# A decoder layer on one core: one more key-half add on VectorE, feed-forward tiles over the score banks, and a new order around the second ln_b pass

## The reference

```python
x = layernorm(x + attention(x))            # 16 heads of 32, q, k, v, o each with a low-rank update
r = scan(ctx * ctx, decay)                 # r_t = decay * r_(t-1) + ctx_t * ctx_t
x = layernorm(x + x * r)
h = silu(bitlinear(x, w1, b1))             # rows rounded to 8 bits, weights to -1, 0, 1; 512 -> 2048
h = gelu(h); h = layer_norm(h) * g + b     # ln_g and ln_b over 2048 columns
x = layernorm(x + bitlinear(h, w2, b2))    # h is rounded to 8 bits again; 2048 -> 512
```

## Time and profile before

| | |
|---|---|
| median of 3 runs | 1042.36 (1042.34 to 1043.55) |
| the profiled execution, its own time | 1039.61 |
| its span, first to last instruction | 1037.8 |
| PE busy | 941.8 (91%) |
| PEld busy | 647.8 (62%) |
| DVE busy | 859.1 (83%) |
| ACT busy | 826.3 (80%) |
| POOL busy | 548.5 (53%) |
| mean granted TensorE clock | 0.966 |

### The profile page before, as it was taken

The page is one execution under the profiler, slowest core; times in us unless marked ns, Lnnn a source line. Parts: engine busy times, 40 slices in busy tenths (PEclk is TensorE's granted clock), DMA queues, the critical chain, the costliest instruction groups (busy, mean ns, idle before and its releaser), DMA issues.

```text
span 1037.8 us, 23337 instructions
## 1 busy us (share of the span) xinstructions
PE 941.8 (91%) x9244; PEld 647.8 (62%) x9260; DVE 859.1 (83%) x1490; ACT 826.3 (80%) x957; POOL 548.5 (53%) x767
## 2 busy tenths in 40 slices
PE   5998987999999999999999999999999999977515
PEld 3766756676777667676767767676767777654102
DVE  4578868889797989889897979898897979897766
ACT  3646686888989798888888897988889897977684
POOL 2332338274654639373755647383746546472643
PEclk9999998999999999999999999999999999999768
DMA  9432200313132222323141212323131412122213
GB/s 361 158 113 113 73 3 21 75 49 88 22 85 52 55 62 56 81 53 85 27 110 22 75 46 61 71 53 85 52 85 22 97 40 75 22 63 54 53 34 89
DMA packets 106351, 73.67 MB, mean 71 GB/s; under 512 B 91385, under 2 KB 91385, under 8 KB 104450
## 3 DMA queue, kind: packets, MB, share of 16 engines
q1 hardware_dynamic: 105522, 70.34, 25.3%
q10 hardware_dynamic: 720, 1.84, 0.5%
HBM read 41.73 MB, written 8.40 MB: 48 GB/s over the span
## 4 chain that ended last, share of the span: by engine, by line
DVE 33%; PE 25%; ACT 17%; issue 13%; POOL 7%; DMA 3%; SPq 1%; DVEq 0%; ACTq 0%; POOLq 0%
PE bank L1484 8%; PE bank L1345 7%; DVE neg_max L965 6%; POOL h L549 5%; DVE stats L1022 3%; ACT h L727 3%; DVE h L1096 3%; ACT junk L737 3%; ACT h L742 3%; DVE fz L1101 2%; DVE qk_parts L988 2%; PE bank L1485 2%; ACT L727 2%; DVE rows L1038 2%; DVE qx L1063 2%
## 5 line engine op out<-in xcount | busy, mean ns | idle before, releaser
L965 DVE TENSOR_REDUCE neg_max<-wave 128x8 f32<-128x2048 f32 x64 | 146.2, 2284 | 29.4 <-PE wave L1370 29.4
L549 POOL TENSOR_TENSOR h<-h,g_tile 128x2048 f32<-128x2048 f32 x30 | 139.2, 4640 | 39.1 <-ACT h L742 39.1
L659 ACT ACTIVATE probs<-wave 128x1024 f32<-128x1024 f32 x128 | 124.2, 1023 | 28.2 <-PE wave L1394 27.9
L1484 PE MATMUL bank<-w,xqT 128*128 128x512 fp8e4 x496 | 130.0, 385 | 17.5 <-DMA xqT<-xq 13.6
L439 POOL TENSOR_SCALAR attn_hi<-attn 128x256 fp32r<-128x256 f32 x64 | 28.3, 442 | 174.3 <-DVE attn L1004 159.4
L697 ACT ACTIVATE rows<-rows,rstd 128x512 f32<-128x512 f32 x96 | 74.4, 807 | 41.9 <-POOL rstd L455 23.7
L1096 DVE TENSOR_TENSOR h<-h,b_tile 128x2048 f32<-128x2048 f32 x32 | 84.1, 2629 | 18.6 <-POOL h L549 18.0
L721 ACT ACTIVATE h<-bank,qx 128x512 f32<-128x512 f32 x124 | 82.3, 689 | 20.0 <-PE bank L1485 16.7
L1491 PE MATMUL bank<-w,hqT 128*128 128x512 fp8e4 x416 | 94.3, 380 | 0.3 <-DMA hqT<-h 0.3
L1484 PEld LDWEIGHTS bank<-w,xqT 128*128 128x128 bf16 x496 | 46.7, 99 | 74.9 <-DMA xqT<-xq 9.9
L1345 PE MATMUL bank<-xT_hi,wq_hi 128*128 128x256 f32 x256 | 78.8, 308 | 0.1
(11 more groups left out here) (184 smaller groups left out, 2736.9 us busy)
## 6 DMA issues: line engine op xcount, KB each, us to landing
ctx_sb<-ctxT SPq DMA_DIRECT2D x16, 512.0 KB, 3.7
rows<-x SPq DMA_DIRECT2D x16, 512.0 KB, 4.0
out<-rows SPq DMA_DIRECT2D x32, 256.0 KB, 2.1
xT_in<-xT SPq DMA_DIRECT2D x15, 512.0 KB, 4.0
h<-w1T SPq DMA_DIRECT2D x4, 1024.0 KB, 14.0
h<-w2T SPq DMA_DIRECT2D x4, 1024.0 KB, 5.0
h<-Wq SPq DMA_DIRECT2D x1, 1024.0 KB, 5.9
h<-Wk SPq DMA_DIRECT2D x1, 1024.0 KB, 9.4
```

Of the source, the lines that this page charges most:

```text
L549: po.tensor_tensor(h_of(b, q)[:, :], h_of(b, q)[:, :], g_tile[:, :], ALU.mult).then_inc(done, 1)
L659: ac.activation(probs[:, kt, :, :], wave[:, :, kt * T:(kt + 1) * T], ACT.Exp, scale=SM_SCALE).then_inc(S["probs_ready"], 1)
L965: dv.tensor_reduce(neg_max[:, :, :], wave[:, :, :].rearrange("p j (t k) -> p j t k", t=NT), axis=AX_X, op=ALU.max, negate=True).then_inc(S ...
L1484: pe.matmul(p[:, :], xqT[:, q, kc, :], w1[:, kc, n * FW:(n + 1) * FW], start=(kc == 0), stop=False)
```

## The change

1. **Row sums of group 3.** A new `add_in_place` on DVE adds the key halves of group 3 into `probs[:, 1]`. It waits for all exponentials of the batch and for the new counter `values_ready`, which PE raises when the matmuls with the values of group 3 are done. The sums are now a function of their own, `summed`; for group 3 it stands behind qk(j+1,1) and reads the added half. `half_added` counts 2 a batch.
2. **Banks of the feed-forward tiles.** 6, 7, 4, 6, 1, 2, 3, 7. Banks 1 to 3 are score banks, so `shifted(j+1,0)`, which writes them, moves from the end of body(j) to behind y in body(j+1), with a wait for the seventh silu. `weighted(b,0)` waits for the third silu in place of the sixth.
3. **DVE's order.** quantise_z(j-2,0) ahead of z_add(j-2,1), add_in_place(j) behind it; scan(j) ahead of quantise_z(j-2,1).
4. **ACT's order.** z_square(j-2,1) behind shiftT(j+1,0), between the two fours of silus.
5. **POOL.** res2 waits for quantise_z(j-3,1), which is now the last of DVE's body, in place of the scan.

```diff
-            (DV, "half_added", 1), (DV, "qk_lo", 8), ...
+            (DV, "half_added", 2), (DV, "qk_lo", 8), ...
+            ... (PE, "values_ready", 1) ...

-        bank_no.update({("f", u): (6, 7, 4)[u % 3] for u in range(8)})
+        bank_no.update({("f", u): (6, 7, 4, 6, 1, 2, 3, 7)[u] for u in range(8)})

 # POOL, body(j)
                     neg_mean(j - 2, 0)
-                    wait(po, "scan_done", j - 1, 5)
+                    if alive(j, 3):
+                        wait(po, "z_quant", j - 3, 12)
+                    else:
+                        wait(po, "scan_done", j - 1, 5)
                     res2(j - 2)

 # ACT, body(j)
                 if alive(j, 2):
-                    z_square(j - 2, 1)
                     zq_store(j - 2, 0)
...
                 if alive(j, -1):
                     qk_hi(j + 1, 1)
                     shiftT(j + 1, 0)
+                if alive(j, 2):
+                    z_square(j - 2, 1)
                 if alive(j, 1):
                     silu(j - 1, 1)

 # DVE
+            def add_in_place(b):
+
+                wait(dv, "probs_ready", b, 8)
+                wait(dv, "values_ready", b, 1)
+                dv.tensor_tensor(probs[:, 1, :, :], probs[:, 0, :, :], probs[:, 1, :, :],
+                                 ALU.add).then_inc(S["half_added"], 1)

 # DVE, lead()
                 maxima(1, 0)
+                add_in_place(0)
                 attn_norm(0, 3)

 # DVE, body(j)
                 if alive(j, 2):
+                    quantise_z(j - 2, 0)
                     z_add(j - 2, 1)
-                    quantise_z(j - 2, 0)
+                add_in_place(j)
                 if j == 1:
                     ternary(7)
...
+                if alive(j, 0):
+                    scan(j)
                 if alive(j, 2):
                     quantise_z(j - 2, 1)
-                if alive(j, 0):
-                    scan(j)

 # PE
             def shifted(b, c):

                 wait(pe, "shiftT_stored", b, c + 1)
+                if c == 0:
+                    wait(pe, "silu_done", b - 2, 7)
...
             def weighted(b, c):
...
                 if c == 0 and b >= 2:
-                    wait(pe, "silu_done", b - 2, 6)
+                    wait(pe, "silu_done", b - 2, 3)
...
+                if c == 3:
+                    last.then_inc(S["values_ready"], 1)
+                else:
+                    summed(b, c)
+
+            def summed(b, c):
+
+                if c in (0, 3):
+                    wait(pe, "half_added", b, 1 if c == 0 else 2)
+                    both = half_sum if c == 0 else probs[:, 1, :, :]
                     for i in range(GH):
-                        last = pe.matmul(bank[4][i * HD:(i + 1) * HD, T:2 * T], ones[:, :], half_sum[:, i, :],
+                        last = pe.matmul(bank[4][i * HD:(i + 1) * HD, T:2 * T], ones[:, :], both[:, i, :],
                                          start=True, stop=True)
...

 # PE, lead()
                 weighted(0, 3)
                 qk(1, 1)
+                summed(0, 3)
                 shiftT(1, 0)
-                shifted(1, 0)

 # PE, body(j)
                 if alive(j, 3):
                     y(j, 0)
+                shifted(j, 0)
...
                 if alive(j, -1):
                     qk(j + 1, 1)
+                summed(j, 3)
...
                 if alive(j, 1):
                     for u in range(NF, 2 * NF):
                         f(j, u)
-                if alive(j, -1):
-                    shifted(j + 1, 0)
```

More of the change, by code:

```diff
@@ L162, in decoder_kernel @@
             (PE, "shifted_ready", 4), (PE, "scores_ready", 4), (PE, "qk_ready", 4), (PE, "v_ready", 2),
-            (PE, "shiftT_ready", 4), (PE, "pv_ready", 4), (PE, "o_ready", 2), (PE, "rT_ready", 2),
+            (PE, "shiftT_ready", 4), (PE, "pv_ready", 4), (PE, "values_ready", 1), (PE, "o_ready", 2), (PE, "rT_ready", 2),
             (PE, "f_ready", 8), (PE, "y_ready", 2),
@@ L170, in decoder_kernel @@
             (AC, "gelu_done", 2), (AC, "h_var", 2), (AC, "h_normed", 2), (AC, "z_squared", 2),
-            (DV, "half_added", 1), (DV, "qk_lo", 8), (DV, "max_done", 4), (DV, "shift_split", 8), (DV, "inverted", 12), (DV, "attn_done", 4),
+            (DV, "half_added", 2), (DV, "qk_lo", 8), (DV, "max_done", 4), (DV, "shift_split", 8), (DV, "inverted", 12), (DV, "attn_done", 4),
             (DV, "scan_done", 5), (DV, "ln1", 6), (DV, "ln2", 6), (DV, "x_quant", 14),
@@ L1407, in weighted @@
                         ch = (GH * c + i) * HD
-                        pe.matmul(bank[4][i * HD:(i + 1) * HD, 0:T], v_sb[b % 2][:, kt, ch:ch + HD], probs[:, kt, i, :],
-                                  start=(kt == 0), stop=(kt == NT - 1))
-                if c == 0:
-                    wait(pe, "half_added", b, 1)
+                        last = pe.matmul(bank[4][i * HD:(i + 1) * HD, 0:T], v_sb[b % 2][:, kt, ch:ch + HD],
+                                         probs[:, kt, i, :], start=(kt == 0), stop=(kt == NT - 1))
+                if c == 3:
[6 more added lines that the diff above has]
+                    both = half_sum if c == 0 else probs[:, 1, :, :]
                     for i in range(GH):
-                        last = pe.matmul(bank[4][i * HD:(i + 1) * HD, T:2 * T], ones[:, :], half_sum[:, i, :],
+                        last = pe.matmul(bank[4][i * HD:(i + 1) * HD, T:2 * T], ones[:, :], both[:, i, :],
                                          start=True, stop=True)
-                for kt in range(NT if c > 0 else 0):
-                    for i in range(GH):
-                        last = pe.matmul(bank[4][i * HD:(i + 1) * HD, T:2 * T], ones[:, :], probs[:, kt, i, :],
-                                         start=(kt == 0), stop=(kt == NT - 1))
+                else:
+                    for kt in range(NT):
+                        for i in range(GH):
+                            last = pe.matmul(bank[4][i * HD:(i + 1) * HD, T:2 * T], ones[:, :], probs[:, kt, i, :],
+                                             start=(kt == 0), stop=(kt == NT - 1))
                 last.then_inc(S["pv_ready"], 1)
```

## The result

The changed kernel takes 1068.99 us in the median, against 1041.09 for the kernel before on the same chip, six runs of each: a ratio of 1.0253, 95% interval 1.0235 to 1.0272. That is slower by 27.9 us, where +21 (1063) was forecast and 1069 was the upper end of the range. The profiled execution grew from a span of 1037.8 to 1067.6, by 29.8.

What follows compares the result with a forecast made beforehand. A ring of waits through PE, ACT, POOL and DVE bounds the kernel, PE within a microsecond. Passes grow 1.47 us, thirteen 19.1, plus 0.7 and 0.9 at the ends: 20.8 on 1042.36, stated 1063; range 1053 to 1069.

Steps and rivals of the forecast that it cites:

- The ring and its terms: Chain of waits round one pass, from quantise_x through tile 3, Gelu load and ln_b: 9.51 + 7.19 + 18.47 + 23.72 = 58.89 us.
- The wait ahead of the sums: On PE behind qk(j+1,1): summed(j,3) waits about 1.6 us for DVE's add; tile 3 starts 0.91 later after quantise_x.
- The saving on PE: Group 3's row sums, 8 instructions for 16: 0.43 us less, about 0.1 lost to a matmul switch, 0.33 a pass.
- PE-bound rival: PE sets the time after all: both PE savings, 0.7 us a pass, are gained, giving 1033 us; chance 6%.
- The square: z_square(j-2,1) between the silus on ACT: tile 3 to Gelu table load takes 7.19 us against 6.54, +0.65 a pass.
- since no silu of theirs held PE up: Feed-forward tiles 4 to 7: own banks 1, 2 and 3 were said to give nothing.
- PE's wait in r(j,1) grows by some 0.6 and meets DVE work that is later still: PE's r(j,1) in each pass: a longer wait, listed among the parts besides the ring's two lengthened terms.
- The clock: PE's granted clock in steady passes: expected to stay at 1.00; a value below that would show the prediction wrong.
- No table load beside the square: ACT, square between two Silus: no table loads counted; if outside Silu's set, two a pass would stand in the ring.
- The ends of the kernel: First pass: add_in_place(1) delays the ternary store, 0.7 us (0 to 1.5); behind the last quantise_x, 0.9 us more.
- The narrow forecast: Kernel time of 1059 to 1067 us, from pass terms between 1.2 and 1.8 us; chance 72%.
- a falling clock: Rival: PE's wait ahead of the tiles lowers its clock; 1085 us, or 1065 to 1075 in a few passes; chance 7%.

Runs made afterwards that it cites:

- e1: The changed kernel with add_in_place(j) moved on DVE between quantise_z(j-2,0) and z_add(j-2,1), 2.21 us earlier: 1048.83 us, ratio 1.0073.
- e5: The changed kernel without the add for group 3 (16 sum instructions as before) and with z_square(j-2,1) back ahead of the silus: 1042.15 us, ratio 1.0002.
- e2: The changed kernel, add included, with z_square(j-2,1) moved on ACT right behind zq_store(j-2,0), ahead of all silus: 1059.4 us, ratio 1.0174.
- e6: The changed kernel with the old feed-forward banks (6, 7, 4), the old silu waits and shifted(j+1,0) at the body's end: 1070.94 us, ratio 1.0277.
- e4: The changed kernel without the new add: group 3's 16 sum instructions as before, all moves and banks kept: 1045.0 us, ratio 1.0038.
- e7: The changed kernel without the add in the first and last batch (0 and 15), whose group 3 keeps 16 sum instructions: 1060.78 us, ratio 1.0182.
- e3: The kernel before with only the add and the later sums, keeping its old banks and orders: 1059.2 us, ratio 1.0177.
- e8: e4 with r(j,1) behind shifted(j,2) on PE and shift_rows of group 2 ahead of h_norm on ACT: 1042.84 us, ratio 1.0012.
- e9: e5 with r(j,1) behind shifted(j,2) on PE and shift_rows of group 2 ahead of h_norm on ACT: 1043.66 us, ratio 1.0024.

## Why the prediction was right, and where it was not

**The ring and its terms: right.** In the pass at 488.79, the operation behind quantise_x starts at 488.76. From there to tile 3 it is 9.52 us (forecast 9.51), to the Gelu table load 7.19 (7.19), to the first ln_b pass 18.51 (18.47), to the next end of quantise_x 23.70 (23.72). The pass is 58.92 against 58.89. Busy times could not have told it: PE's in one pass hardly moved, 56.84 against 56.76, while the pass grew by 1.5. e1 shows that the first of the terms is due to the place of the add and not to the add as such.

**The wait ahead of the sums: right, a little large.** 1.36 was measured, 1.5 to 1.6 forecast, and DVE's idle 0.76 where some 0.7 was forecast.

**The saving on PE: in the rows of the sums, not in PE's busy time.** The prediction counted 0.33 a pass. The 8 sums do take 0.57 (494.46 to 495.03) in place of the 0.97 of the earlier trace rows. But over the 13 passes PE is busy for 733.20 us, against 733.02 before. Nor does it show without the wait: e1, with the adds, has 734.42, and e5, with the 16 sums, 734.34. Busy times of matmuls have modelled ends, but the two kernels share that. What takes the saving back stays open. So the part of the PE-bound rival's gain that was to come from the sums is not seen, whatever the ring allowed.

**The square: right in the changed kernel, for a reason that I had only in part.** It costs 0.53 (e2), where the forecast had 0.65 from the term tile 3 to table load, and the sum was right because the 0.13 by which e2's path is longer than the old 6.54 is not on the changed kernel's ring. I had written that the tiles' own banks give nothing, "since no silu of theirs held PE up". That was true of the order before; with the square in between it isn't: e6 shows 0.30 a pass without them. The sum had them in it without saying so, since it took PE's tiles 4 to 7 as done before ACT gets to them, which only the new banks allow. I should have asked what is late next if the banks stay.

**"PE's wait in r(j,1) grows by some 0.6 and meets DVE work that is later still": right here, wrong as a view of the margin.** It is 0.72 us at 532.11 and harmless in the changed kernel, because the first ring is longer. But without the add (e4) and with the add early (e1) that very wait holds the pass at 57.74. The prediction's rival of a PE-bound 1033, which took both savings of PE as a gain, happened in no kernel here: the shortest passes are 57.42 and 57.45 and not 56.7. Half of PE's idle time is this wait for DVE.

**The clock: right.** It stayed at 1.00 from 200 to 930 us, with waits of 1.31 to 1.73 us ahead of the sums in twelve passes. The Trainium skill, on its page TensorE: Matmul & The Clock Gate (section A second HAM failure mode: psum-queue depth-cycling), tells of a kernel in which short idle times between groups of matmuls made the clock swing; by the row of the pass at 488.79 that doesn't happen here. In the last pass the clock is at its lower level, 1.2 GHz, behind PE's wait of 6.56 us (columns as in the earlier trace rows):

```profile
966.20:969.50 3.30, 3.30 (x12) 1.19 (x9) 3.03 (x5) 0.69 (x1) 1.13 (x2) 0.50 0.47 91
```

But this is nothing that the change brought. The kernel before falls to it at the same place, 0.57 over 937.15 to 940.47, behind a wait of 3.56 us for xqT, and e7 is at it there too, 0.50 over 956.84 to 960.00 (tile 0 takes 1.86). The change only sets the sums into that stretch as well, 1.08 in place of 0.64.

**No table load beside the square: right.** ACT's rows have none between 501.12 and 503.01. By the page ScalarE: Activation LUTs of the Trainium skill (section Table sets: the hidden batching unit) one was possible, since it doesn't say where Square belongs; the trace shows that it runs within Silu's set. The load that there is, ahead of Gelu, took 1.28 us in the changed kernel.

**The ends of the kernel: the step that failed.** The prediction's own terms add up to 20.7 (19.1, 0.7 and 0.9; it says 20.8), and the median moved by 27.9. In the profiled executions of before and changed the difference is 29.8, stretch by stretch:

| stretch | before | after | difference | forecast |
|---|---|---|---|---|
| start to maxima(1,0) | 71.87 | 74.57 | 2.70 | none |
| to the scan (the add of lead()) | 12.48 | 14.27 | 1.79 | none |
| to the first transpose | 39.04 | 40.32 | 1.28 | none |
| to the second (add_in_place(1)) | 63.82 | 64.26 | 0.44 | 0.7 |
| 13 passes | 746.45 | 766.13 | 19.68 | 19.1 |
| last pass to the drain's | 40.98 | 44.60 | 3.62 | 0.9 |
| to the end | 63.16 | 63.45 | 0.29 | none |

- The last pass, 3.62 instead of 0.9 (3.23 against e7). I took the end of the add as 5.66 behind quantise_x there too, which is right (965.16 less 959.51 is 5.65), but compared it with a start of the tiles of the steady kind. In the last pass PE has no projection ahead of them, so without the add they start when xqT lands: 3.52 after the transpose in e7, and 3.49 in the kernel before (937.15 less 933.66). That row was there to be read, and with it the step would have given 6.3 less 3.5, 2.8.
- The add of lead(), 1.8 us. It wasn't in the sum at all; I had counted only add_in_place(1).
- add_in_place(1): 0.7 (0 to 1.5) was forecast. It starts at 131.12, behind the first transpose, so its cost lies between the first transpose and the second. That stretch grew by 0.44, and by 0.30 in e7, which has this add too. The store of the earlier trace rows does start 3.1 us later behind the first transpose than before, but little of that reaches the second.
- Two stretches grew that have no added operation in them. Ahead of maxima(1,0) all kernels run the same program, and these maxima start at 71.17 and 71.51 in e3 and e6, which have the add as well. From the scan to the first transpose it is 40.32, but also 40.68, 40.19 and 40.09 in e5, e8 and e9, which have no add. The granted clock is 0.87 there in these and 0.91 in the kernels with 39.0 to 39.1. All five kernels with the add of lead() have 0.87, and three of the seven without, so that this add makes the lower clock likelier is neither shown nor excluded. The stretch in e7 and e5 (columns of the earlier trace rows):

```profile
84.27:123.39 39.12, 32.27 (x366) 24.56 (x368) 32.20 (x65) 27.98 (x35) 12.39 (x21) 0.91 0.23 82
```

```profile
83.42:124.11 40.69, 33.85 (x366) 25.93 (x368) 32.35 (x66) 27.98 (x35) 12.40 (x21) 0.87 0.21 79
```

So the forecast was 7.1 us short in the median. The last pass was sized 2.7 too small, lead() 1.8 and the passes 0.6, add_in_place(1) 0.3 too large, and 0.3 is the drain's, for which I have no cause. That is 5.1; the other 2 are of the size by which the start varies. The narrow forecast of 1059 to 1067, which had 72%, was missed. That the whole range held the time, with its last 0.01 us, was luck: its upper end had been drawn for a falling clock, which is not what filled it.

## What to carry to other kernels

Where engines run fixed orders, follow the ring of waits round one pass and sum its terms; an operation is then priced by the place it takes in the ring, not by its duration: the same 1.22 us add costs 1.2 us a pass in one place (58.93 against 57.74 in e4, without it) and nothing in another, 2.2 us earlier (57.75). When an edit shortens one ring, look for the next in the small waits that cost nothing so far (here 0.3 us at r(j,1)), for they mark the rings that are nearly as long. And price the first and the last pass from their own rows, since the work that hides a wait in the steady passes isn't there: two of sixteen adds went with 7 to 8 of the 28 us.

## What the runs showed of the hardware that I had not expected

- **The start of the kernel varies with the same program.** The maxima of batch 1 start between 70.95 and 74.57 us in the profiled executions, though nothing ahead of them differs. One cause is where the clock is at its lower level: in the stretch 33 to 42 us it was 0.74 in the changed kernel and 1.00 in e7, with PE busy all the time in both. So differences of some 3 us between two profiled executions say nothing here; medians are needed. The stretch in the changed kernel (columns of the earlier trace rows):

```profile
33.00:42.00 9.00, 9.00 (x63) 7.69 (x63) 2.33 (x7) 6.49 (x7) 3.92 (x1) 0.74 0.36 123
```

And in e7:

```profile
33.00:42.00 9.00, 9.00 (x71) 7.77 (x71) 4.62 (x8) 8.74 (x10) 4.63 (x1) 1.00 0.39 122
```

- **Some DVE operations and POOL's passes take turns: the one that starts second ends late.** In each steady pass of the changed kernel, POOL's L498 now runs beside the scaling of ctx (L1026) and the first small product of the scales of h (L1130, one column). The first takes 1.41 us in the mean of 16, against 0.69 before, and the second 0.65 in the mean of 30, against 0.19 before; together 25.5 us of DVE's busy time. DVE's timeline:

```profile
504.76 1.57 DVE L1026 TENSOR_SCALAR ctx_sb<-ctx_sb 128x1024 f32<-128x1024 f32 x1
506.25 1.22 DVE L1130 TENSOR_TENSOR fz<-fz 128x1 f32<-128x1 f32 x1
```

POOL's of the same pass:

```profile
504.46 3.00 POOL L498 TENSOR_TENSOR rows<-rows,bo_tile 128x512 f32<-128x512 f32 x2
```

Overlap alone doesn't do it. In e4 and e8 the two overlap in 13 passes as well, but there DVE's operation starts 0.28 us before POOL's L498, where in the changed kernel it starts 0.30 behind it. It then takes 0.69, as alone, and it is the first instruction of L498 that grows, from 1.26 to 1.53. DVE's timeline in e4:

```profile
490.76 0.69 DVE L1026 TENSOR_SCALAR ctx_sb<-ctx_sb 128x1024 f32<-128x1024 f32 x1
```

POOL's:

```profile
491.04 2.76 POOL L498 TENSOR_TENSOR rows<-rows,bo_tile 128x512 f32<-128x512 f32 x2
```

At the start of the changed kernel, behind attn_norm(0,3), the two engines alternate:

```profile
82.07 4.50 POOL L498 TENSOR_TENSOR rows<-rows,bo_tile 128x512 f32<-128x512 f32 x2
```

The ternary operation at 85.35 (L1161) starts inside the second instruction of this row, which ends at 86.57, and ends 1.09 us behind it: 2.32, against 1.27 at 81.82 in e7, where POOL is idle. Not every operation takes part. In the kernel before, z_max (L1101, a reduction) runs beside L498 in 13 passes and takes 2.28, as alone, and the instructions of L498 keep their 1.26 to 1.28. So the engines wait for each other not only by semaphores, as the section on the chip has it, but also inside an instruction. What the two share is not seen in these traces, and no run was made for it; that the order of the starts decides is read from e4 and e8 against the changed kernel.
